# Window attention and an MLP on one Trainium2 core: scores and weighted sums over all 128 rows, block-diagonal, with a reordered turn

## What is computed

```python
qkv = xw @ qkv_w.T + qkv_b                 # windows of 16 tokens, 64 channels
qn, kn = q / norm(q), k / norm(k)
attn = softmax(einsum('whnd,whmd->whnm', qn, kn) * scale + bias + mask)
out = einsum('whnm,whmd->whnd', attn, v) @ proj_w.T + proj_b
x = x + layernorm(out) * g1 + o1
x = x + layernorm(gelu(x @ fc1_w.T + b1) @ fc2_w.T + b2) * g2 + o2
# layer 1, for each channel: moving average (25) + filtered rest (128 modes, complex weights)
```

## Time and profile before

| | |
|---|---|
| profiled execution, device time | 8510.45 us |
| its span | 8508.3 us |
| median of the runs | 8508.97 us |
| TensorE matmul busy | 8028.3 us (94%), 293684 instructions |
| TensorE weight loads | 5317.5 us (62%) |
| VectorE | 5495.2 us (65%) |
| ScalarE | 6156.0 us (72%) |
| GpSimd | 5157.8 us (61%) |
| DMA | 834.40 MB, mean 98 GB/s |

### The profile page before, as it was taken

One profiled execution on the slowest core, in us unless ns is written; L12 is line 12 of the kernel. 1 busy time (PEld: TensorE's weight loads), 2 busy tenths in 40 slices (PEclk: granted clock), 3 DMA queues, 4 the chain that ended last, 5 costly groups with the idle time before them and its releaser, 6 DMA issues.

```text
span 8508.3 us, 658585 instructions
## 1 busy us (share of the span) xinstructions
PE 8028.3 (94%) x293684; PEld 5317.5 (62%) x293684; DVE 5495.2 (65%) x8029; ACT 6156.0 (72%) x8530; POOL 5157.8 (61%) x5127
## 2 busy tenths in 40 slices
PE   8899999999999999999999999999999999878786
PEld 5556666666666666666666666666666666667675
DVE  1467777777777777777777777777777777322221
ACT  1478888888888888888888888888888888422221
POOL 0367777777777777777777777777777777100000
PEclk9799999999999999999999999999999999989898
DMA  3122222222222222222222222222222222699999
GB/s 99 52 50 59 58 58 59 59 59 58 58 58 57 56 58 59 59 58 58 59 59 58 58 59 59 59 58 58 56 56 58 59 59 58 202 357 331 359 331 336
DMA packets 1187119, 834.40 MB, mean 98 GB/s; under 512 B 633233, under 2 KB 1043217, under 8 KB 1182867
## 3 DMA queue, kind: packets, MB, share of 16 engines
q1 hardware_dynamic: 1182404, 698.61, 31.9%
q10 hardware_dynamic: 4608, 134.22, 3.7%
HBM read 412.97 MB, written 285.21 MB: 82 GB/s over the span
## 4 chain that ended last, share of the span: by engine, by line
PE 73%; SPq 14%; DMA 7%; issue 4%; ACT 1%; DVE 0%; ACTq 0%; POOL 0%; POOLq 0%; DVEq 0%
PE ps L501 12%; PE ps L479 11%; SPq L335 10%; PE ps L581 9%; PE ps L542 9%; PE ps L554 9%; PE ps L462 8%; PE ps L526 5%; PE ps L513 5%; DMA out<-arena 4%; DMA arena<-in_x 3%; PE ps L450 3%; SPq L346 2%; SPq L341 2%; PE ps L424 1%
## 5 line engine op out<-in xcount | busy, mean ns | idle before, releaser
L953 POOL TENSOR_TENSOR arena<-arena 128x512 f32<-128x512 f32 x1024 | 1043.2, 1040 | 886.3 <-PE ps L501 886.3
L479 PEld LDWEIGHTS ps<-arena 32*32 32x32 f32 x131072 | 1236.8, 106 | 511.5 <-issue 503.6
L501 PEld LDWEIGHTS ps<-arena 32*32 32x32 f32 x131072 | 1288.5, 103 | 289.1 <-issue 256.4
L501 PE MATMUL ps<-arena 32*32 32x16 f32 x131072 | 1422.7, 186 | 19.0 <-issue 17.4
L479 PE MATMUL ps<-arena 32*32 32x16 f32 x131072 | 1346.9, 180 | 24.8 <-issue 18.0
L985 POOL TENSOR_TENSOR arena<-arena 128x512 f32<-128x512 f32 x512 | 712.9, 1392 | 950.0 <-DVE arena L844 950.0
L805 DVE TENSOR_TENSOR arena<-ps,arena 128x768 f32<-128x768 f32 x1024 | 980.8, 958 | 358.7 <-PE ps L462 346.8
L462 PEld LDWEIGHTS ps<-arena 64*128 64x128 f32 x8192 | 648.4, 188 | 837.0 <-issue 829.9
L694 ACT ACTIVATE arena<-ps,arena 128x1024 f32<-128x1024 f32 x1024 | 1137.8, 1111 | 6.5
L581 PE MATMUL ps<-xch,amat 128*128 128x256 f32 x4096 | 911.4, 386 | 241.7 <-ACT arena L718 195.0
L542 PE MATMUL ps<-arena 64*128 64x512 f32 x4096 | 1031.5, 621 | 2.8 <-ACT arena L682 2.3
(11 more groups left out here) (89 smaller groups left out, 13925.4 us busy)
## 6 DMA issues: line engine op xcount, KB each, us to landing
arena<-in_x SPq DMA_DIRECT2D x4096, 32.0 KB
arena<-arena SPq DMA_DIRECT2D x1024, 128.0 KB, 2.3
y<-ystripe SPq DMA_DIRECT2D x256, 512.0 KB
amat<-mix SPq DMA_DIRECT2D x512, 256.0 KB, 3.4
xch<-y SPq DMA_DIRECT2D x512, 256.0 KB, 4.1
out<-arena ACTq DMA_DIRECT2D x32, 4096.0 KB, 27.1
mix<-amat SPq DMA_DIRECT2D x64, 256.0 KB, 2.0
wri<-in_w_real SPq DMA_DIRECT2D x64, 64.0 KB, 1.8
```

The costliest lines, as they stand in the source:

```text
L479: ins = mm(S(sl)[r, c0 + e:c0 + 32:2], qT[r, sl, q, e:64:2], kT[r, sl, q, e:32:2], start=True, stop=True, tile_position=(32 * cg, 32 * cg))
L501: ins = mm(PV[32 * h:32 * h + 32, b, c0:c0 + N], vexp[r, sl, h, :, :], pT[r, sl, h // 2, h % 2, :], start=True, stop=True, tile_position=( ...
L953: tt(vexp.rearrange("p s h e d -> p (s h) e d")[:, :, e, :], qkv[ring(g, 4)][:, 2].rearrange("p s (h d) -> p (s h) d", h=HEADS), par[:, e: ...
```

## The change: what it does

The block-diagonal form. k and the softmax output, transposed in blocks of 32 rows, are copied by DMA (`spread_k`, `spread_p`, four DMAs of 64 KB each) into `kTx` and `pTx`, buffers of 128 rows by 2,048 columns that are zero outside of their diagonal blocks. `scores` and `weighted` then take all 128 rows in one matmul for a 32-column tile, with 64 columns moved: 32 matmul statements each in a turn instead of 128 each, on four column tiles.

Around it: x is loaded by two DMAs of 128 KB instead of eight, its transposed form has two buffers, and a DMA (`copy_x`, 256 KB) keeps it for the residual; GpSimd's two additions of offsets go (`add_o1`, `add_o2`), and the offsets move into the gelu's bias and `gain2`. The qkv projection is split in `project_qk` and `project_v`, whose input VectorE regroups (`regroup_x`); `qk_out` (1,024 elements a row) and `v_out` (a copy of 512) take the place of the two bias additions of 768. The two logarithms of the norms become one instruction of 1,024, and so do the two roots. PSUM: scores in bank 4, weighted sums in bank 5, where the transposed x goes as well, and the variances in banks 4 and 5. The lag becomes 10 turns, TensorE's loop holds four turns instead of one, VectorE's eight instead of four. The squares of q and k stay on ScalarE and are first in its turn, then `keep_o` and the two gelus.

```diff
-LAG = 7
-SWAP = 4
+LAG = 10
...
+        kTx = rows[:, 0:2048].rearrange("p (c s q t) -> p c s q t", c=4, s=SLOTS, q=2)
+        pTx = rows[:, 2048:4096].rearrange("p (c q x h n) -> p c q x h n", c=4, q=2, x=SLOTS, h=2)
...
-        PV = ps[:, 4:6, 0:256]
+        SB, PV = ps[:, 4, :], ps[:, 5, :]
...
-        VV = MB
+        VV = ps[:, 4:6, :]
...
+        XT = PV
...
-                need(sp, xT_ps, before(g))
-                for a in range(2):
-                    src = xr[bass.ds(s * ROWS, ROWS)][:, a * HALF + q * QW:a * HALF + q * QW + QW, :]
-                    for p in range(4):
-                        sp.dma_start(xin[:, p, a * C:a * C + C], src[:, p * 8:p * 8 + 8, :]).then_inc(x_in, 16)
+                if there(g):
+                    need(sp, xT_ps, before(g))
+                    for a in range(2):
+                        src = xr[bass.ds(s * ROWS + q * WIN, WIN)][:, a * HALF:(a + 1) * HALF, :]
+                        sp.dma_start(xin[:, :, a * C:a * C + C], src.rearrange("r p c -> p r c")).then_inc(x_in, 16)
+
+            def copy_x(g):
+                if there(g):
+                    need(sp, xT_sb, g)
+                    sp.dma_start(xr8[ring(g, 8)], xT[ring(g, 2)]).then_inc(xr_in, 16)
+
+            def spread_p(g):
+                if there(g):
+                    need(sp, pT_sb, g)
+                    for c in range(4):
+                        r = slice(32 * c, 32 * c + 32)
+                        sp.dma_start(pTb[r, c, :], pT[r, :]).then_inc(pTx_in, 16)
...
+            def spread_k(g):
+                if there(g):
+                    need(sp, kT_sb, g)
+                    for c in range(4):
+                        r = slice(32 * c, 32 * c + 32)
+                        sp.dma_start(kTb[r, c, :], kT[r, :]).then_inc(kTx_in, 16)
...
+            def turn(b, k):
+                copy_x(Group(b, k - 1))
+                spread_p(Group(b, k - 5))
+                swap_halves(Group(b, k - 7))
+                spread_k(Group(b, k - 3))
...
+                    turn(d * 8, k)
                     if k % GPS == 0:
-                        store_y(d * 2 + (k // GPS - 3), Group(d * 8, k - 12 + GPS - 1))
-            for i in range(G, G + 9):
-                swap_halves(Group(i, -SWAP))
+                        store_y(d * 2 + (k // GPS - 4), Group(d * 8, k - 16 + GPS - 1))
...
-                        after(pe, (gelu0, i6), (l1_sb, i5, i7), (xT_sb, before(g)))
+                        need(pe, x_in, g, 16 * 2)
+                        after(pe, (oT_sb, i6), (xT_sb, before(g)))
...
+                def project_qk(g):
+                    if there(g):
+                        need(pe, xT_sb, g)
+                        after(pe, (gelu0, i9), (qk_sb, before(g)))
+                        for p in range(4):
+                            for a in range(2):
+                                ins = mm(MA[:, a, p * P:(p + 1) * P], xT[ring(g, 2)][a * C:a * C + C, p * P:(p + 1) * P],
+                                         wqkv[a * C:a * C + C, 0:2 * C], start=True, stop=True, tile_position=(a * C, 0))
+                        ins.then_inc(qk_ps, 1)
+
+                def project_v(g):
+                    if there(g):
+                        need(pe, xTc_sb, g)
+                        after(pe, (gelu1, i9), (vb_sb, before(g)))
+                        for c in range(4):
+                            for a in range(2):
+                                ins = mm(MB[:, a, c * C:(c + 1) * C],
+                                         xTc[a * C:a * C + C, c * P:(c + 1) * P],
+                                         wqkv[a * C:a * C + C, 2 * C:3 * C], start=True, stop=True, tile_position=(a * C, 0))
+                        ins.then_inc(v_ps2, 1)
...
-                        if part == 0:
-                            need(pe, qT_sb, g)
-                            need(pe, kT_sb, g)
-                            after(pe, (oT_sb, i4), (biased, before(g)))
-                            settled(pe)
-                        for sl in range(part * 4, part * 4 + 4):
+                            need(pe, biased, before(g))
+                        settled(pe)
+                        sv = SB.rearrange("p (q a c m e) -> p q a c m e", q=2, a=2, c=4, e=2)
+                        for a in range(2):
                             for q in range(2):
                                 for e in range(2):
-                                    c0 = SC(sl) + q * 32
-                                    for cg in range(4):
-                                        r = slice(32 * cg, 32 * cg + 32)
-                                        ins = mm(S(sl)[r, c0 + e:c0 + 32:2], qT[r, sl, q, e:64:2],
-                                                 kT[r, sl, q, e:32:2], start=True, stop=True,
-                                                 tile_position=(32 * cg, 32 * cg))
-                        if part == 1:
-                            ins.then_inc(S_ps, 1)
-
-                def weighted(g, d, done):
-                    if there(g):
-                        if d == 0:
-                            need(pe, pT_sb, g)
-                            need(pe, v0_sb, g)
-                            need(pe, v1_sb, g)
-                            after(pe, (biased, i2), (oT_sb, before(g)))
+                                    for p in range(4):
+                                        ins = mm(sv[32 * p:32 * p + 32, q, a, :, :, e], qT[:, a * 4 + p, q, e:64:2],
+                                                 kTx[:, :, a * 4 + p, q, e:32:2], start=True, stop=True,
+                                                 tile_position=(0, 32 * p))
+                        ins.then_inc(S_ps, 1)
...
+                def weighted(g):
+                    if there(g):
+                        need(pe, pTx_in, g, 16 * 4)
+                        need(pe, v0_sb, g)
+                        need(pe, v1_sb, g)
+                        if there(i8) or there(i10):
+                            need_norms(pe, l12_sb, i8, i10)
                         else:
-                            need(pe, pvA_ps, g)
+                            need(pe, oT_sb, before(g))
+                            need(pe, xT_sb, i1)
                         settled(pe)
-                        for sl in range(SLOTS):
-                            c0 = (sl // 2 % 2 * 4 + sl // 4 * 2 + sl % 2) * 32 + d * N
-                            for h in range(HEADS):
-                                for b in range(2):
-                                    cg = 2 * b + d
-                                    r = slice(32 * cg, 32 * cg + 32)
-                                    ins = mm(PV[32 * h:32 * h + 32, b, c0:c0 + N], vexp[r, sl, h, :, :],
-                                             pT[r, sl, h // 2, h % 2, :], start=True, stop=True,
-                                             tile_position=(32 * cg, 32 * h))
-                        ins.then_inc(done, 1)
+                        ov = PV.rearrange("p (a s c n) -> p a s c n", a=2, s=4, c=4)
+                        for a in range(2):
+                            for c in range(4):
+                                for h in range(HEADS):
+                                    ins = mm(ov[32 * h:32 * h + 32, a, :, c, :], vexp[:, a * 4 + c, h, :, :],
+                                             pTx[:, :, h // 2, a * 4 + c, h % 2, :], start=True, stop=True,
+                                             tile_position=(0, 32 * h))
+                        ins.then_inc(pv_ps, 1)
...
-                        after(pe, (xT_sb, i0), (gelu0, i6), (l1_sb, before(g), before(h)))
+                        need(pe, biased, i4)
+                        after(pe, (xT_sb, i0), (oT_sb, i6))
+                        if not (there(i4) and there(i6)) and (there(i8) or there(i10)):
+                            need_norms(pe, l12_sb, i8, i10)
...
-                scores(i2, 0)
-                project(i4)
+                first_layer(i9, 0, MA, fc1a_ps)
+                first_layer(i9, 1, MB, fc1b_ps)
+                weighted(i6)
+                scores(i4)
                 turn_x(i0)
-                scores(i2, 1)
-                second_layer(i6, 0, fc2a_ps)
-                second_layer(i6, 1, fc2b_ps)
-                project_qkv(i0, 0, MA, qkvA_ps)
-                weighted(i3, 0, pvA_ps)
-                variances(i4, i6)
-                project_qkv(i0, 1, MA, qkvB_ps)
-                weighted(i3, 1, pvB_ps)
-                first_layer(i5, 0, MB, fc1a_ps)
-                first_layer(i5, 1, MA, fc1b_ps)
-
-            over_groups(pe, step, 1)
+                project(i7)
+                second_layer(i9, 0, fc2a_ps)
+                second_layer(i9, 1, fc2b_ps)
+                project_qk(i1)
+                project_v(i1)
+                variances(i7, i9)
+
+            over_groups(pe, step, 4)
...
+                        need(act, qk_ps, before(g, 2))
+                        need(act, xr_in, before(g), 16)
```

(81 more changed lines are left out.)

257 lines of the change are left out of this document (102 added, 155 removed).

## The result

The changed kernel takes 8835.68 us, median of four runs (8810.42 to 8871.56), beside 8510.15 us for the kernel before on the same chip: a ratio of 1.0386 (95% interval 1.0349 to 1.0423). It is slower, where I forecast 7970 us and a range of 7650 to 8420. The profiled execution took 8837.18 us, its span 8835.4 us. The time lies in the attention loop, not at its ends.

The account below looks back on a forecast made before the run. TensorE's own list bounded the kernel at 13.52 us a turn; after the change, a chain of 11.95 plus 0.6 for the store gives 12.55. Sum: 465 + 495 x 12.55 + 102 + 1189 + 2 = 7970 us, range 7650 to 8420.

Parts of the forecast that it names:

- rival (d): TensorE's four-turn loop, about 1,640 instructions, does not stay loaded: 1.6 us more a turn, 8762 us; chance 0.06.
- The term for the store: Every fourth turn the store of y delays the load of x by 2.4 us: 0.6 us a turn.
- The chain: Dependencies through several engines, from the variances' end to their next end, set the attention turn: 11.95 us.
- ScalarE's part: Within the chain, logarithms, roots, table load, square of q and k and `keep_o`: done at 5.1 us.
- the second: Second loop of the chain, through `keep_o`, gelus, square1, swap of halves and variances: 11.3 to 11.9 us.
- the first loop: ScalarE to `keep_o`, then turn_x, project, second layer, q and k, v, variances: 11.95 us with hand-overs.
- Rival (a): The store of y does no harm: 11.9 to 12.3 us a turn, 7650 to 7850 us; chance 0.25.
- TensorE's sizes: Stage times in TensorE's list after the change, scores and weighted 1.46 us each; sum 11.44 us a turn.
- Rival (c): Weight loads hide behind no matmul: scores and weighted 2.5 us each, 8540 us; chance 0.07.
- SP's queue: 13.5 issues a turn, 7.7 us; x lands near 14.7, cover 2.4 us, late only behind the store.
- "I count none": No price for a lowered granted clock on TensorE after an idle stretch near 3 us.
- The ends: Outside the loop: T16 at 465 us, 102 us after T511, channel stage 1189, 2 outside the span.

Follow-up runs that it names:

- e4: The changed kernel with the first instruction of TensorE's four-turn loop at place 0 of a program block; 8,294 us.
- e10: The changed kernel with TensorE's loop head at place 0 and the store of y cut into two 512 KB transfers two turns apart, both behind `copy_x`; 7670.96 us.
- e7: e5 with the square of q and k covering 64 of its 1,024 columns; 8019.13 us.
- e6: The changed kernel with TensorE's loop head at instruction 200 of a fetch block, nothing else changed; 9200.97 us.
- e12: e6 with a fetch hint on the back edge of TensorE's loop; 8297.58 us.
- e2: The changed kernel with the store of y issued early in SP's turn, behind `copy_x`, instead of just ahead of the next load of x; 8365.76 us.
- e5: e4 with e2's place of the store; 7887.52 us.

## Why the prediction was wrong, point by point

**The step that failed.** The sum had no term for fetching TensorE's instructions: it let the loop of four turns stay loaded, and rival (d), which did not, was given 0.06. Measured, that is 1.09 us a turn, worth 542 us. With the code kept loaded and nothing else changed (e4) the time is 8,294 us, high but inside the range. The term for the store, 0.6 us a turn where 1.25 was measured, is the second error; alone it would not have put the time outside of the range.

**The chain was right, its figure in part by luck.** I added 11.95 us a turn from rows of the kernel before. Measured are 11.94 in an undisturbed turn of the changed kernel and 11.99 as the mean of e10. ScalarE's part, 5.1 us from the end of the variances to `keep_o`, is 4010.85 to 4015.90, 5.05 us. But the loop that closes the turn is not the one that I summed to 11.95. It is the second, over the gelus, `square1` and the swap, which I had at 11.3 to 11.9:

```profile
4017.82 0.69 ACT L693 ACTIVATE arena<-ps,arena 128x512 f32<-128x512 f32 x1
```
```profile
4018.54 1.14 SPq L351 DMA_DIRECT2D arena<-arena  x2
```

The swap goes out when `square1` is done, and the variances stand 0.31 us waiting for it, until 4021.66, 11.96 us after those of the turn before. Without that wait the first loop would be about 11.6 us (an estimate, 11.94 - 0.31): q and k took 0.99 us in it where I gave 1.27. Rival (a) put 7674 us on a turn of 11.95; e10 has 7671, since its `turn_x` of 16 comes 34 us earlier than in my sum, and the turns and the end are some 34 us longer. The square is on the chain: without it the turn is 11.45 us (e7), and VectorE comes next.

**TensorE's sizes were too high, without effect.** Scores and weighted at 1.46 us each were charged with a fixed part for four tiles; the weighted sums take 0.92 (4012.66 to 4013.58). That is 57 ns for each of 16 passes, 53 of them columns, so the loads of four tiles are hidden almost wholly, though one of them lasts 114 ns:

```profile
L534 PEld LDWEIGHTS ps<-rows,arena 128*32 128x32 f32 x32768 | 510.3, 114 | 451.3 <-issue 451.2
```

Rival (c) fell with this. By the rule of the Trainium skill ("TensorE: Matmul & The Clock Gate", Part 3), that a load overlaps a running matmul only when the row groups differ, none of the four loads would be hidden. With the same page's columns/1.2 ns for a load (Part 2) a pass would then be 107 ns, an estimate from that page; the trace, with 57 ns, does not agree. First layer, weighted sums and scores end before ScalarE's 5.1 us are over in any case, so the error only shows as idle time ahead of `turn_x`, 1.3 us instead of 0.3.

**SP's queue was mis-sized, 0.6 instead of 1.25 us a turn.** e4 against e10: 13.24 - 11.99 = 1.25 us, or 5.0 us for each store, just the upper end that I had written down. Three errors are in the 0.6. By my own figures x was 2.7 us late and not 2.4 (14.7 + 5.1 - 17.1). In e4 its turn is 3.3 us too long. And "I count none" for the clock was the largest: the turn behind the wait costs another 2.2 us, at half clock, in the passage shown (the 5.5 us of that passage are a little above the mean of 5.0). Chance (a) had half of the truth: the queue can be ordered so that the store does no harm (e10), but not in the order that the change has.

**Rival (d) happened, at two thirds of its price.** I gave it 0.06. Its reason was right (the body of four turns doesn't stay loaded); its price of 1.6 us a turn was not, the changed kernel pays 14.33 - 13.24 = 1.09, or 4.4 us a pass in the mean, as some 2.9 us of standing at the head in the passes that fetch, the half clock behind it and what that makes late. These passes are 6.6 us longer than e4's, the others 1.5. e6, where every pass fetches, pays 9201 - 8294 = 907 us, 1.8 us a turn. What I set against (d) was the Trainium skill ("Runtime: NRT & Kernel Launch", Instruction fetch mechanics), which gives TensorE room for 2,048 instructions, refilled in blocks of 256; here the traces agree with the block (11.14 MB / 680 = 16.4 KB, its 16 KiB) but not with what I made of the room. A body of 1,639 instructions lies in 7 such blocks if it starts in the first 154 places of one and in 8 if it starts later; where the changed kernel's own head stands, no run here shows. At place 0 it stayed (41 packets), at its own place and at 200 it did not (680 and 1,140). I had compared 1,640 with 2,048 and stopped there. It is tempting to say that 8 blocks are one too many, but e12 stands against it: from place 200, in 8 blocks, the body stayed once the branch back carried the hint. So the room is not what fails by itself; what counts is place and branch together. What is fetched or dropped at the branch, and why the changed kernel's own place fetches in about every other pass only, no run here settles.

**The ends were nearly right.** T16 at 432 instead of 465, with 11.6 us for each of the turns 4 to 15 where I gave 12, and 1,311 us from `turn_x` of 511 to the span's end instead of 1,291.

**The sum again**, with what the runs gave: 432 + 495 x (11.99 + 1.25 + 1.09) + 1311 + 2 = 8838 us, against 8837 of the profiled execution. It has to agree, since the three terms are differences of the same traces; it shows where the time is and is no test. The two terms together are more than the gain of 13.52 - 11.99 = 1.53 us a turn. They don't quite add (e2 and e4 save 470 and 542 us alone, e5 948 together). And the 1.09 holds one thing more than the stop: in the changed kernel the swap is waited for up to 2.4 us in the turn after it, and in e4, with 41 packets, never over 0.4. The trace ties this to the fetches. From 1000 to 7000 us the 531 swap transfers with no packet of queue q8 (instructions) in flight beside them landed 2.2 to 2.4 us after their issue; of the 303 beside such a packet 126 took over 3 us, up to 4.4. In e4 all 906 took 2.2 to 2.4. Whether and how a packet of 16 KB holds up a transfer, no run of its own shows.

## What to carry to other kernels

When a change lengthens a loop body, count its instructions and where its head falls in the blocks of the program, and look at the profile page's packets of instructions before reading anything else: 680 instead of 41 is a result by itself, and here aligning the head or hinting the back edge was one line of code. In a queue that works in order, cut a large store into pieces smaller than the cover of what stands behind it, and follow the buffer that it releases as well as the transfers that it delays. Price every new idle stretch of TensorE with the clock behind it: here a load of x that was 3.3 us late cost about 5.

## What the runs showed of the hardware

Not expected: the place of a loop's head alone, with the same body of 1,639 instructions, moves the time from 8,294 to 9,201 us (e4, e6), and a hint at the back edge brings it back at the worst place (8,298 us, e12). The granted clock was 0.50 behind waits of 2.92 us (changed kernel), 3.33 (e7) and 4.42 (e4), each time for the next 3 us of matmuls or more. Behind the wait of 2.92 us it fell only when matmuls ran again; in the two longer ones it fell during the wait (0.89 from 3019 to 3022.3 us in e7, 0.86 from 4046 to 4051 in e4). Behind a wait of 2.29 us in the changed kernel it was 0.50 as well (4040.2 to 4043 us), while the waits of about 1 us (1.4 at most) in every turn of e10 left it at 1.00. In e5 the mean behind a wait of 2.05 us was 0.64 (3024 to 3027 us), behind one of 1.95 us 1.00 (4018 to 4022). And four 64 KB transfers issued behind 1 MB on the same queue took 4.5 to 5.4 us to issue instead of 2.4 (e5, e7): the issues are held up as well, not only the data.
